# Rounded weights of the delta rule: GpSimd makes them per unit from raw weights, no longer per head in the table stage

## The chip, the cores and the metric

The kernel runs on one core of a Trainium2 chip. The metric is the device time of one execution in microseconds (us); a comparison takes the median of several executions. The engines are TensorE (PE in the views; PEld is its loading of weights), VectorE (DVE), ScalarE (ACT), GpSimd (POOL) and SyncE (SP), which here only issues transfers.

## What is computed

Input x has 8 sequences of 512 rows and 256 columns. Four blocks follow one another, each added to its own input:

```python
x = x + attn_a(layernorm(x))   # gated delta rule, 8 heads of 128, two key/value steps per row
x = x + ffn(layernorm(x))      # 256 -> 512 -> 512 -> 256, ReLU
x = x + attn_b(layernorm(x))   # attention, 16 heads, 4 key/value heads
x = x + ffn(layernorm(x))
```

The change concerns attn_a alone:

```python
q = silu(conv(x @ Wq)); k = silu(conv(x @ Wk)); v = silu(conv(x @ Wv))   # causal conv, 4 taps
q = l2norm(q) / sqrt(128); k = l2norm(k)
beta = 2 * sigmoid(x @ Wb); g = -exp(A_log) * softplus(x @ Wa + dt_bias)
for each row:                                   # per head, a state of 128 x 128
    state = state * exp(g)
    for j in (0, 1):
        state = state + k_j (v_j - k_j state)^T * beta_j
    o = q state
out = (rmsnorm(o) * norm_w * silu(x @ Wg)) @ Wo
```

## The kernel before

It is written engine by engine, with semaphores. Five stages run one after the other: `build_tables` (the table stage), `delta_rule`, a feed-forward stage, the second attention, and a feed-forward stage again. Within a stage each engine works through its own fixed list of instructions.

**float32 products in pieces.** A factor is split into a rounded piece `hi` (type float32r) and the rest, `lo` = value - `hi`; a product is hi*hi + hi*lo + lo*hi. In `project`, six matmuls (L571) make one 128 x 512 block from `w_hi`, `w_lo`, `x_hi` and `x_lo`.

**The table stage** loops over the 8 batches. VectorE takes statistics (L311), normalizes in four instructions of 128 x 256 (L320), TensorE transposes (L250), ScalarE copies the result out (L281, and rounded at L283), VectorE makes `lo` (L326), SP stores both pieces to xs_d in memory. VectorE waits for L283 before L326, so it begins the next batch behind it. Beside this loop GpSimd has its own over the heads' weights (`split_head`): SP loads a head's raw weights (128 x 1536, `load_head`), GpSimd multiplies by one into the rounded `wh_hi` (L230) and subtracts into `wh_lo` (L232), and SP stores both to ws_d (`store_head`, L179). There are nine such heads, the first one twice. Behind the loops come the gates (L330 to L352, beta and g for all heads) and one store of the tables, tab_d.

**The delta rule stage** loops over 64 units, a batch and a head each (`units`, `turn`); two batches of 8 units are one run of the loop. Sequences are cut into 8 chunks of 64 rows, 128 key rows each. In the turn of unit u TensorE, VectorE and ScalarE interleave three things by hand: the projections, convolutions and transposes of unit u, the levels of the inverse of a triangular matrix per chunk, and the chain over the chunks of an earlier unit (`chain_ks`, `chain_u`, `chain_s`: key times state, the update u, the new state). The parts that the prediction speaks of:

- SP's list per turn: the store of oT, the tables' row of the next unit (`g_tab`, L510), the weights of the next unit (`g_w_hi`, `g_w_lo`, L514, 768 KB each, and `g_taps`), then L stored to lower_d (L527) and read back as 16 x 16 blocks (`g_small`, L529), the inverted blocks stored (L535, 64 KB each), and read back as T (L538) and U (L540), 512 KB each. `sp.wait_ge` holds this list in order.
- GpSimd's list per turn (L1161 on): `g_dmt` masked (L1165), the sums for the next unit from `g_tab` (L1143, L1144), `bk2` (L1169, it needs the key norms that VectorE makes at L1045 and L1046), `g_dm` (L1170), `g_ctab` (L1171, L1172), then the substitution in the 16 x 16 blocks (L1152, L1154, some 30 short instructions) which waits for `g_small`, and `g_qg` (L1177).
- VectorE makes L from the Gram blocks and `g_dm` (L1011), and does the convolution's taps (L962).
- At the start GpSimd clears tiles (L1181, L1183), waits for VectorE's zeros (`d_zero2`) and raises the starting values of the semaphores (L1188).

Of the kernel before, what the change touches and what calls it, by code (L numbers as in the profile page):

```python
# [107 lines left out]
def build_tables(nc, io, sems):  # L108
# [3 lines left out]
    with ExitStack() as ctx:  # L112
# [51 lines left out]
        def _(sp):  # L164
# [8 lines left out]
            def load_head(h, par):  # L173
                sp.dma_start(wh[par][:], io["w_heads"][bass.ds(h, 1)].rearrange("a p k n c -> p (a k n) c")).then_inc(s[f"t_wh{par}"], 16)

            def store_head(h, par):
                sp.wait_ge(s["t_split"], 2 * h + 2)
                for i, piece in enumerate((wh_hi, wh_lo)):
                    sp.dma_start(io["ws_d"][bass.ds(h, 1), i:i + 1].rearrange("a i p n c -> p (a i n) c"),  # L179
                                 piece[par][:].bitcast(F32)).then_inc(s[f"t_ws{par}"], 16)  # L180

# [37 lines left out]
        @block.gpsimd  # L219
        def _(pool):  # L220
            nc.gpsimd.memset(eps[:], LN_EPS).then_inc(s["t_init"], 1)
            nc.gpsimd.memset(tab[:], 0.0).then_inc(s["t_init"], 1)
# [11 lines left out]
            pool.wait_ge(s["t_const"], 48)  # L234
            with pool.Fori(0, H // 2) as pair:
                for par in (0, 1):
                    split_head(pair * 2 + par, pair, par)
            split_head(H, H // 2, 0)
# [60 lines left out]
        def _(dve):  # L299
# [65 lines left out]
def delta_rule(nc, io, sems):  # L365
# [3 lines left out]
    with ExitStack() as ctx:  # L369
# [126 lines left out]
        def _(sp):  # L496
# [64 lines left out]
        def _(pe):  # L561
# [272 lines left out]
        def _(act):  # L834
# [43 lines left out]
            def turn(u, q, pair=None, b=None, hp=None, own=True, inverse=True):  # L878
# [48 lines left out]
                if own:  # L927
# [19 lines left out]
        def _(dve):  # L947
# [70 lines left out]
            def turn(u, q, pair=None, b=None, hp=None, own=True, inverse=True, base=None):  # L1018
# [1389 lines left out]
```

## Time and profile before

| | us |
|---|---|
| median of 3 runs | 4455.96 (4451.16 to 4456.58) |
| the profiled execution, its own time | 4464.27 |
| its span, first to last instruction | 4462.2 |
| table stage | 0 to 170 |
| delta rule stage | 170 to 2561 |
| mean granted clock of TensorE | 0.973 of full speed |

The profile is of one execution. Busy time in it is per engine and stage; an instruction's idle time before it is given with what released it, and a transfer with the time from its issue to its landing. In a timeline row the first number is the start and the second the time from the start to the end of the group in it.

### The profile page before, as it was taken

What the parts mean: (1) busy time and instruction counts of PE and PEld (TensorE: products, weight loads), DVE (VectorE), ACT (ScalarE), POOL (GpSimd) and SP (SyncE); (2) the same over time, 40 slices, a digit from 0 to 9 for tenths busy, and PEclk for the clock granted to TensorE, in tenths of its full rate; (3) what the DMA queues carried; (4) which work ended last, traced back from release to release, by engine and by line L of the source; (5) the groups of instructions that cost most, each with busy time, mean ns of one, the idle gap of its engine ahead of it and who ended that gap; (6) DMA issues with size and microseconds to landing.
All of it is one profiled execution on the core that took longest, in us unless ns stands there. A gap on an engine that the chain in (4) does not pass through costs nothing. (4 is left out here: it accounts for less than half of the span.)

```text
span 4462.2 us, 97071 instructions
## 1 busy us (share of the span) xinstructions
PE 4129.1 (93%) x32143; PEld 3442.7 (77%) x32143; DVE 3010.4 (67%) x7897; ACT 2183.5 (49%) x5660; POOL 1201.0 (27%) x2727
## 2 busy tenths in 40 slices
PE   3499999999999999999999779879999999999979
PEld 3388888888888888888888668767777777778768
DVE  5577777777777777777777345346776776776655
ACT  2255555555555555555555234334444444444344
POOL 5244444444444444444444100000000000000000
PEclk9999999999999999999999689979999999999989
DMA  6433433333333343333333132131111111111021
GB/s 253 150 100 101 120 114 106 106 102 109 100 110 99 107 123 106 104 110 100 109 100 101 59 134 85 41 98 41 38 51 52 52 32 52 52 47 42 15 68 34
DMA packets 558447, 393.06 MB, mean 88 GB/s; under 512 B 253040, under 2 KB 504944, under 8 KB 556400
## 3 DMA queue, kind: packets, MB, share of 16 engines
q1 hardware_dynamic: 557936, 386.69, 28.1%
q8 instruction: 267, 4.37, 0.4%
q14 instruction: 244, 2.00, 0.2%
HBM read 288.36 MB, written 98.14 MB: 87 GB/s over the span
## 5 line engine op out<-in xcount | busy, mean ns | idle before, releaser
L962 DVE SCALAR_TENSOR_TENSOR g_conv<-g_r,g_taps,g_conv 128x511 f32<-128x511 f32 (+2 forms) x961 | 700.0, 742 | 135.9 <-ACT g_conv L847 127.6
L851 ACT ACTIVATE g_us<-g_chn 128x128 f32<-128x128 f32 x528 | 146.6, 278 | 688.4 <-PE g_chn L646 687.6
L2001 ACT ACTIVATE a_pr<-a_pr,a_low 128x128 f32<-128x128 f32 (+3 forms) x512 | 286.6, 560 | 396.2 <-DVE a_low L2146 380.3
L1152 POOL TENSOR_TENSOR g_prod<-g_small 64x14 f32<-64x14 f32 (+6 forms) x896 | 227.0, 253 | 665.8 <-DMA g_small<-lower_d 600.2
L571 PE MATMUL g_r<-g_x_hi,g_w_hi 128*128 128x512 f32 x770 | 366.9, 477 | 9.6 <-issue 7.1
L2146 DVE CUSTOM_DVE_ANT_0 a_pr<-a_sc,a_bias 128x128 f32<-128x128 f32 (+3 forms) x512 | 242.2, 486 | 193.2 <-issue 174.2
L2306 POOL TENSOR_TENSOR a_dg<-a_const,a_fl 128x384 fp32r<-128x384 f32 x32 | 26.4, 826 | 1154.5 <-DVE a_fl L2153 1154.5
L571 PE MATMUL g_r<-g_x_hi,g_w_lo 128*128 128x512 f32 x770 | 306.8, 398 | 0.0
L571 PE MATMUL g_r<-g_x_lo,g_w_hi 128*128 128x512 f32 x770 | 305.0, 396 | 0.0
L1820 PE MATMUL a_out<-a_pt,a_v 128*128 128x512 f32 (+3 forms) x1024 | 297.9, 434 | 0.9 <-DVE a_oT L2166 0.9
L847 ACT ACTIVATE g_conv<-g_r,g_taps 128x512 f32<-128x512 f32 x321 | 220.4, 687 | 137.4 <-PE g_r L571 127.0
L1820 PEld LDWEIGHTS a_out<-a_pt,a_v 128*128 128x128 f32 x1024 | 185.0, 191 | 103.1 <-issue 62.6
L995 DVE SCALAR_TENSOR_TENSOR g_R<-g_chn,g_ctab,g_bv 128x128 f32<-128x128 f32 x462 | 160.4, 347 | 150.9 <-PE g_chn L638 136.7
L1154 POOL TENSOR_TENSOR g_small<-g_small,g_prod 64x14 f32<-64x14 f32 (+6 forms) x896 | 240.6, 269 | 70.3
L1828 PE MATMUL a_pb<-a_wo,a_oT 128*128 128x256 f32 x1024 | 231.8, 379 | 1.7 <-DVE a_oT L2166 0.9
L1003 DVE SCALAR_TENSOR_TENSOR g_S<-g_S,g_ctab,g_chn 128x128 f32<-128x128 f32 x396 | 137.2, 346 | 134.7 <-PE g_chn L656 134.7
L646 PE MATMUL g_chn<-g_R,g_U 128*128 128x128 f32 x924 | 213.9, 314 | 8.3 <-DVE g_R L995 6.9
L638 PE MATMUL g_chn<-g_S,g_kT 128*128 128x128 f32 x924 | 205.1, 304 | 13.8 <-DVE g_S L1001 10.9
L658 PE MATMUL g_ob<-g_us,g_at 128*128 128x128 f32 x1056 | 214.6, 286 | 0.4 <-ACT g_us L851 0.4
L987 DVE TENSOR_TENSOR g_U<-g_U,g_lev 64x128 f32<-64x128 f32 x520 | 147.8, 284 | 93.7 <-PE g_lev L611 88.2
L1828 PEld LDWEIGHTS a_pb<-a_wo,a_oT 128*128 128x128 f32 x1024 | 189.7, 190 | 25.3 <-DVE a_x L2186 1.2
L1745 PE MATMUL a_sc<-a_k_hi,a_q_hi 128*128 128x128 f32 (+3 forms) x512 | 185.4, 362 | 25.6 <-DVE a_low L2146 19.0
(355 smaller groups left out, 11714.6 us busy)
## 6 DMA issues: line engine op xcount, KB each, us to landing
g_w_hi<-ws_d SPq DMA_DIRECT2D x65, 768.0 KB, 5.5
g_w_lo<-ws_d SPq DMA_DIRECT2D x65, 768.0 KB, 6.7
lower_d<-g_L SPq DMA_DIRECT2D x64, 512.0 KB, 3.3
g_T<-low_d SPq DMA_DIRECT2D x64, 512.0 KB, 4.1
g_U<-upp_d SPq DMA_DIRECT2D x64, 512.0 KB, 5.4
a_w<-w_groups SPq DMA_DIRECT2D x32, 640.0 KB, 4.5
oT_d<-g_oT SPq DMA_DIRECT2D x67, 256.0 KB, 5.4
f_oT<-oT_d SPq DMA_DIRECT2D x8, 2048.0 KB, 9.4
```

The costliest lines, as they stand in the source:

```text
L571: mm = M.matmul(BANK[n][:], a[:, k, n, :], c[:, k, :], start=(i == 0), stop=(i == len(terms) - 1))
L638: M.matmul(chn[:, 0, :], keys[:, c, :], S[c % 2][:], start=True, stop=True).then_inc(s["d_ks"], 1)
L646: M.matmul(chn[:, 1, :], U[par][:, c, :], bv[par][:, 0, :] if c == 0 else R[:], start=True, stop=True).then_inc(s["d_u"], 1)
L658: mm = M.matmul(dst, at[(q + 2) % QN][:, c, :], us[:], start=(c % 2 == 0), stop=False)
L847: A(conv[TURN[n] % 2][:], BANK[n][:], ACT.Copy, scale=taps[par][:, n, CONV - 1:CONV]).then_inc(s["d_tap"], 1)
L962: ins = V.scalar_tensor_tensor(out=y[:, k:L], in0=x[:, 0:L - k], scalar=tap, in1=y[:, k:L], op0=ALU.mult, op1=ALU.add)
L1152: ch.link(G.tensor_tensor(prod[:, 0:SM - 1 - k, 0:k], small[:, k + 1:SM, k:k + 1].to_broadcast(shape), small[:, k:k + 1, 0:k].to_broadcast ...
L1154: ch.link(G.tensor_tensor(rest, rest, prod[:, 0:SM - 1 - k, 0:k], ALU.subtract))
L1820: mm = M.matmul(out[:, k * P:L], v[bp][:, k, at], pt[g % 2][:, first[k]:first[k] + L - k * P], start=(k == 0), stop=(k == TT - 1))
L1828: mm = M.matmul(pb[:, j * D:(j + 1) * D], oT[tp_][:, g, m * P:(m + 1) * P], wo[tp_][:, g, :], start=(g == 0), stop=(g == G - 1))
L2001: A(pr[g % 2][:, i, 0:width(i)], pr[g % 2][:, i, 0:width(i)], ACT.Exp, scale=-1.0, bias=low[g % 2][:, i:i + 1], accum_out=tot[g % 2][:, i: ...
L2146: V.tensor_tensor_reduce(pr[g % 2][:, i, 0:width(i)], sc[i % 2][:, 0:width(i)], bias[tp_][:, i, 0:width(i)], -SCALE, 3.0e38, ALU.add, ALU. ...
```

## The change

The table stage no longer handles heads' weights: `load_head`, `store_head` and `split_head` are gone, with their tiles and semaphores, and ws_d with them. The delta rule stage has a new tile `g_w_raw` (128 x 1536). SP loads a unit's raw weights from the input, two units ahead; GpSimd makes `w_hi` and `w_lo` of the next unit from it in every turn (`split_w`), 65 times in all with the first unit, whose `w_hi` is a copy by ScalarE and whose `w_lo` is made by GpSimd before its loop. TensorE waits for `d_wlo` instead of the transfer. The core of the diff:

```diff
@@ build_tables, gpsimd
-            def split_head(h, pair, par):
-                pool.wait_ge(s[f"t_wh{par}"], 16 * pair + 16)
-                pool.wait_ge(s[f"t_ws{par}"], 32 * pair + 1)
-                nc.gpsimd.tensor_tensor(wh_hi[par][:], wh[par][:], cc["ones"].unsqueeze(1).to_broadcast([P, KD * NB, P]), ALU.mult).then_inc(s["t_split"], 1)
-                pool.wait_ge(s["t_split"], 2 * h + 1)
-                nc.gpsimd.tensor_tensor(wh_lo[par][:], wh[par][:], wh_hi[par][:], ALU.subtract).then_inc(s["t_split"], 1)
...
@@ delta_rule, sync
-            def weights(h, par):
-                for i, piece in enumerate((w_hi, w_lo)):
-                    sp.dma_start(piece[par][:].rearrange("p k n c -> p (k n) c").bitcast(F32),
-                                 io["ws_d"][bass.ds(h, 1), i:i + 1].rearrange("a i p n c -> p (a i n) c")).then_inc(s[f"d_w{par}"], 16)
-                sp.dma_start(taps[par][:], io["taps"][bass.ds(h, 1)].rearrange("a p n t -> p (a n) t")).then_inc(s[f"d_w{par}"], 16)
+            def weights(h):
+                sp.dma_start(w_raw[:], io["w_heads"][h % H]).then_inc(s["d_wr"], 16)
+
+            def tap_rows(h, par):
+                sp.dma_start(taps[par][:], io["taps"][h % H]).then_inc(s[f"d_w{par}"], 16)
...
                 tables(u + 1, 1 - par)
-                sp.wait_ge(s["d_proj"], NB * u + 1)
                 sp.wait_ge(s["d_conv"], 5 * u + 1)
-                weights(hp * QN + q + 1, 1 - par)
+                tap_rows(hp * QN + q + 1, 1 - par)
...
                 for i, name in enumerate(("low_d", "upp_d")):
                     sp.dma_start(blocks_of(name), inv[:, i]).then_inc(s["d_XT"], 16)
+                sp.wait_ge(s["d_wlo"], u + 2)
+                weights(hp * QN + q + 2)
...
             rows(0)
+            sp.wait_ge(s["d_wlo"], 1)
+            weights(1)
             sp.wait_ge(s["d_zero2"], 1)
...
@@ delta_rule, tensor
-                    pe.wait_ge(s[f"d_w{1 - par}"], 48 * (pair + par) + 48)
+                    pe.wait_ge(s["d_wlo"], u + 2)
...
@@ delta_rule, scalar
+            act.wait_ge(s["d_wr"], 16)
+            A(w_hi[0][:], w_raw[:], ACT.Copy).then_inc(s["d_whi"], 1)
...
@@ delta_rule, gpsimd
+            def split_w(u, par):
+
+                raw, ones = w_raw[:].rearrange("p k n c -> p (k n) c"), cc["ones"].unsqueeze(1).to_broadcast([P, KD * NB, P])
+                pool.wait_ge(s["d_wr"], 16 * u + 16)
+                pool.wait_ge(s["d_proj"], NB * (u - 1) + 1)
+                hi, lo = (x[par][:].rearrange("p k n c -> p (k n) c") for x in (w_hi, w_lo))
+                G.tensor_tensor(hi, raw, ones, ALU.mult).then_inc(s["d_whi"], 1)
+                pool.wait_ge(s["d_whi"], u + 1)
+                G.tensor_tensor(lo, raw, hi, ALU.subtract).then_inc(s["d_wlo"], 1)
...
                 G.tensor_tensor(ctab[q][:, 1, :], tab[par][:, 2, :], cc["ones"][:, 0:NC], ALU.mult)
+                split_w(u + 1, 1 - par)
                 substitute(u)
...
+            pool.wait_ge(s["d_whi"], 1)
+            G.tensor_tensor(w_lo[0][:], w_raw[:], w_hi[0][:], ALU.subtract).then_inc(s["d_wlo"], 1)
             pool.wait_ge(s["d_zero2"], 1)
```

GpSimd's list in a turn of the delta rule, before (an ISA row stands for a wait; g_bk and g_rk are bk2 and rk2):

```order
L1169 TENSOR_TENSOR g_bk<-g_tab,g_rk 128x8
L96 ISA
L1170 TENSOR_TENSOR g_dm<-g_dm,g_bk 128x512
L1171 TENSOR_TENSOR g_ctab<-g_tab,g_rk 128x8
L1172 TENSOR_TENSOR g_ctab<-g_tab,g_const 128x8
L1148 ISA
L1152 TENSOR_TENSOR g_prod<-g_small 64x14
```

and with the change:

```order
L1155 TENSOR_TENSOR g_bk<-g_tab,g_rk 128x8
L96 ISA
L1156 TENSOR_TENSOR g_dm<-g_dm,g_bk 128x512
L1157 TENSOR_TENSOR g_ctab<-g_tab,g_rk 128x8
L1158 TENSOR_TENSOR g_ctab<-g_tab,g_const 128x8
L1125 ISA
L1126 ISA
L1128 TENSOR_TENSOR g_w_hi<-g_w_raw,g_const 128x1536
L1129 REGISTER_ALU
L1130 TENSOR_TENSOR g_w_lo<-g_w_raw,g_w_hi 128x1536
L1134 ISA
L1138 TENSOR_TENSOR g_prod<-g_small 64x14
```

The two splits stand between the last g_ctab and the first instruction that needs g_small; line numbers are lower by 14 there.

SP's list in a turn, from the tables' row on, before:

```order
L510 DMA g_tab<-tab_d 128x40
L523 ISA
L524 ISA
L514 DMA g_w_hi<-ws_d 128x1536
L514 DMA g_w_lo<-ws_d 128x1536
L516 DMA g_taps<-taps 128x20
L526 REGISTER_ALU
L527 DMA lower_d<-g_L 128x8x128
L528 ISA
L529 DMA g_small<-lower_d 64x16x16
L535 DMA low_d<-g_inv 64x16x16
L535 DMA upp_d<-g_inv 64x16x16
L536 REGISTER_ALU
L537 ISA
L538 DMA g_T<-low_d 128x8x128
L539 ISA
L540 DMA g_U<-upp_d 128x8x128
```

and with the change:

```order
L479 DMA g_tab<-tab_d 128x40
L492 ISA
L485 DMA g_taps<-taps 128x20
L494 REGISTER_ALU
L495 DMA lower_d<-g_L 128x8x128
L496 ISA
L497 DMA g_small<-lower_d 64x16x16
L503 DMA low_d<-g_inv 64x16x16
L503 DMA upp_d<-g_inv 64x16x16
L504 REGISTER_ALU
L482 DMA g_w_raw<-w_heads 128x1536
L506 ISA
L507 ISA
L508 DMA g_T<-low_d 128x8x128
L509 ISA
L510 DMA g_U<-upp_d 128x8x128
```

The two loads of weights behind g_tab are gone, and the raw load stands between the inverse's stores and T.

## Rows read from the trace of the kernel before

**Rows 1.** The page, busy time, share of the span and instructions of TensorE
```profile
PE 4129.1 (93%) x32143; PEld 3442.7 (77%) x32143; DVE 3010.4 (67%) x7897; ACT 2183.5 (49%) x5660; POOL 1201.0 (27%) x2727
```

**Rows 2.** Windows: length, then each engine's busy us, TensorE's clock, DMA share, GB/s
```profile
0.00:170.00 170.00, 53.51 (x330) 43.61 (x330) 88.85 (x150) 35.20 (x47) 64.30 (x31) 1.00 0.60 221
...
300.00:2300.00 2000.00, 1976.52 (x19255) 1656.75 (x19254) 1498.94 (x3404) 1135.88 (x3185) 871.09 (x2169) 1.00 0.36 107
```

**Rows 3.** Groups of the table stage: busy us, mean ns, then idle before
```profile
L320 DVE TENSOR_SCALAR t_xn<-t_x,t_mv,t_rstd 128x256 f32<-128x256 f32 x32 | 40.6, 1269 | 1.2
```

**Rows 4.** Single lines of VectorE: duration in ns, min/median/max, first and last start
```profile
L320 DVE TENSOR_SCALAR t_xn<-t_x,t_mv,t_rstd x32: 411/415/3458, 13.9 to 114.0; 128x256 f32<-128x256 f32 x32
...
L962 DVE SCALAR_TENSOR_TENSOR g_conv<-g_r,g_taps,g_conv x961: 732/741/752, 194.2 to 2485.5; 128x511 f32<-128x511 f32 x65, 128x509 f32<-128x509 f32 x64, 128x510 f32<-128x510 f32 x64
...
L1011 DVE TENSOR_TENSOR g_L<-g_lev,g_dm x128: 679/681/692, 208.7 to 2466.0; 128x512 f32<-128x512 f32 x128
...
L1045 DVE TENSOR_SCALAR g_ss<-g_ss x64: 160/658/1047, 204.5 to 2461.3; 128x8 f32<-128x8 f32 x64
```

**Rows 5.** Timeline, first batches: start us, us, engine, line; GpSimd, then VectorE
```profile
12.89 3.42 POOL L230 TENSOR_TENSOR t_wh_hi<-t_wh,t_const 128x1536 fp32r<-128x1536 f32 x1 [9.65 <-DMA t_wh<-w_heads]
...
23.30 3.42 POOL L232 TENSOR_TENSOR t_wh_lo<-t_wh,t_wh_hi 128x1536 fp32r<-128x1536 f32 x1
...
13.90 12.96 DVE L320 TENSOR_SCALAR t_xn<-t_x,t_mv,t_rstd 128x256 f32<-128x256 f32 x4
...
32.03 1.80 DVE L311 BATCH_NORM_STATS2 t_stats<-t_x 128x6 f32<-128x256 f32 x4
...
34.83 1.76 DVE L320 TENSOR_SCALAR t_xn<-t_x,t_mv,t_rstd 128x256 f32<-128x256 f32 x4
...
41.77 1.80 DVE L311 BATCH_NORM_STATS2 t_stats<-t_x 128x6 f32<-128x256 f32 x4
```

**Rows 6.** DMA issues of 0 to 195 us: KB, median us to landing
```profile
t_x<-x SPq DMA_DIRECT2D x8, 512.0 KB, 4.5
```

**Rows 7.** Timeline, start of the delta rule stage: SP's queue, then GpSimd
```profile
171.30 0.42 SPq L514 DMA_DIRECT2D g_w_hi<-ws_d  x1
...
180.47 0.20 POOL L1183 MEMSET g_qden<- 128x4 f32 x4
...
184.04 0.82 POOL L1188 MEMSET g_scrap<- 128x1 f32 x23 [3.38 <-DVE g_scrap L1122]
```

**Rows 8.** DMA issues of 300 to 2300 us: KB, median us to landing
```profile
g_w_hi<-ws_d SPq DMA_DIRECT2D x56, 768.0 KB, 5.5
...
g_taps<-taps SPq DMA_DIRECT2D x56, 10.0 KB, 7.3
```

**Rows 9.** Waits of 300 to 2300 us: total, times, longest
```profile
POOL g_prod L1152 <- DMA g_small<-lower_d: 522.8, 56, 10.4
```

**Rows 10.** Timeline of a unit (GpSimd, VectorE), and the narrowest wait for g_small
```profile
1277.93 1.04 POOL L1170 TENSOR_TENSOR g_dm<-g_dm,g_bk 128x512 f32<-128x512 f32 x1
...
1279.10 0.20 POOL L1172 TENSOR_TENSOR g_ctab<-g_tab,g_const 128x8 f32<-128x8 f32 x1
...
1288.62 0.21 POOL L1152 TENSOR_TENSOR g_prod<-g_small 64x14 f32<-64x14 f32 x1 [9.32 <-DMA g_small<-lower_d]
...
1280.92 1.28 DVE L1011 TENSOR_TENSOR g_L<-g_lev,g_dm 128x512 f32<-128x512 f32 x2
...
789.33 0.21 POOL L1152 TENSOR_TENSOR g_prod<-g_small 64x14 f32<-64x14 f32 x1 [7.27 <-DMA g_small<-lower_d]
```

**Rows 11.** Timeline of SP's queue in the same unit
```profile
1265.06 0.68 SPq L535 DMA_DIRECT2D upp_d<-g_inv  x1
...
1268.24 0.39 SPq L538 DMA_DIRECT2D g_T<-low_d  x1
```

**Rows 12.** Windows around it: the last number is what the DMA engines moved, GB/s
```profile
1267.00:1269.00 2.00, 2.00 (x13) 1.52 (x12) 1.93 (x5) 0.99 (x3) 0.00 (x0) 1.00 0.11 14
...
1274.00:1277.00 3.00, 3.00 (x27) 2.96 (x27) 2.61 (x5) 2.21 (x13) 1.74 (x2) 1.00 1.05 428
```

More of the change, by code:

```diff
@@ L145, in build_tables @@
         start = sb("t_start", [P, 8])
-        wh = [sb(f"t_wh{i}", [P, KD * NB, P]) for i in (0, 1)]
-        wh_hi, wh_lo = ([sb(f"t_wh_{n}{i}", [P, KD * NB, P], F32R) for i in (0, 1)] for n in ("hi", "lo"))
         ps_x = ps("t_ps_x", [P, 2, L])
@@ L171, in load_x @@
                 sp.dma_start(x[par][:], io["x"][bass.ds(b, 1)].rearrange("a (m p) d -> p (a m) d", p=P)).then_inc(s[f"t_x{par}"], 16)
[L173 to L180, printed above, removed]
             def store_rows(b, par):
@@ L192, in turn @@
                 store_rows(b, par)
-                store_head(b, par)
-                if more or par == 0:
-                    load_head(b + 2, par)
             load_x(1, 1)
-            load_head(0, 0)
-            load_head(1, 1)
             with sp.Fori(0, B // 2 - 1) as pair:
@@ L205, in _ @@
             store_rows(B, 1)
-            store_head(H, 0)
-            sp.wait_ge(s["t_ws0"], 32 * (H // 2 + 1) + 1)
-            sp.wait_ge(s["t_ws1"], 32 * (H // 2) + 1)
             sp.wait_ge(s["t_glo"], 1)
@@ L222, in _ @@
             nc.gpsimd.memset(tab[:], 0.0).then_inc(s["t_init"], 1)
-            for i, name in enumerate(("t_out0", "t_out1", "t_tr", "t_sig", "t_ws0", "t_ws1", "t_xlo")):
+            for i, name in enumerate(("t_out0", "t_out1", "t_tr", "t_sig", "t_xlo")):
                 nc.gpsimd.memset(start[:, i:i + 1], 0.0).then_inc(s[name], 1)
-            def split_head(h, pair, par):
-                pool.wait_ge(s[f"t_wh{par}"], 16 * pair + 16)
-                pool.wait_ge(s[f"t_ws{par}"], 32 * pair + 1)
-                nc.gpsimd.tensor_tensor(wh_hi[par][:], wh[par][:], cc["ones"].unsqueeze(1).to_broadcast([P, KD * NB, P]), ALU.mult).then_inc(s["t_split"], 1)
-                pool.wait_ge(s["t_split"], 2 * h + 1)
-                nc.gpsimd.tensor_tensor(wh_lo[par][:], wh[par][:], wh_hi[par][:], ALU.subtract).then_inc(s["t_split"], 1)
[L234 to L238, printed above, removed]
         @block.tensor
@@ L356 @@
 T_SEMS = ["t_const", "t_x0", "t_x1", "t_xT", "t_out0", "t_out1", "t_tab", "t_init", "t_xn", "t_tr", "t_ab", "t_g", "t_sum", "t_A",
-          "t_mv", "t_std", "t_sig", "t_beta", "t_abs", "t_exp", "t_dec", "t_dve", "t_wh0", "t_wh1", "t_ws0", "t_ws1", "t_split", "t_xlo", "t_xhi", "t_glo", "t_move"]
+          "t_mv", "t_std", "t_sig", "t_beta", "t_abs", "t_exp", "t_dec", "t_dve", "t_xlo", "t_xhi", "t_glo", "t_move"]
 K0, K1, V0, V1, QB, GB = range(6)
@@ L385, in delta_rule @@
         x_hi, x_lo = (sb(f"g_x_{i}", [P, KD, L], F32R) for i in ("hi", "lo"))
+        w_raw = sb("g_w_raw", [P, KD, NB, P])
         w_hi, w_lo = (some(2, f"g_w_{i}", [P, KD, NB, P], F32R) for i in ("hi", "lo"))
@@ L540, in turn @@
                 sp.dma_start(U[par][:], chunks_of("upp_d")).then_inc(s["d_TU"], 16)
-            weights(0, 0)
+            weights(0)
+            tap_rows(0, 0)
             tables(0, 0)
             rows(0)
+            sp.wait_ge(s["d_wlo"], 1)
+            weights(1)
             sp.wait_ge(s["d_zero2"], 1)
@@ L554, in _ @@
                 store(u)
-            sp.wait_ge(s["d_w0"], 48 * (UNITS // 2 + 1))
+            sp.wait_ge(s["d_w0"], 16 * (UNITS // 2 + 1))
+            sp.wait_ge(s["d_wr"], 16 * (UNITS + 2))
             sp.wait_ge(s["d_tab0"], 16 * (UNITS // 2 + 1))
@@ L825, in _ @@
             pe.wait_ge(s["d_x"], 32)
-            pe.wait_ge(s["d_w0"], 48)
+            pe.wait_ge(s["d_wlo"], 1)
             pe.wait_ge(s["d_at"], 1)
@@ L931, in turn @@
                     ins.then_inc(s["d_qsq"], 1)
-                    act.wait_ge(s[f"d_w{1 - par}"], 48 * (pair + par) + 48)
+                    act.wait_ge(s[f"d_w{1 - par}"], 16 * (pair + par) + 16)
                     first_tap(u + 1, 1 - par, K0)
                     A(tiny[:], tiny[:], ACT.Silu)
+            act.wait_ge(s["d_wr"], 16)
+            A(w_hi[0][:], w_raw[:], ACT.Copy).then_inc(s["d_whi"], 1)
             act.wait_ge(s["d_zero"], 1)
@@ L939, in _ @@
             decay_start(0, 0)
-            act.wait_ge(s["d_w0"], 48)
+            act.wait_ge(s["d_w0"], 16)
             first_tap(0, 0, K0)
@@ L1104, in turn @@
                 if own:
-                    dve.wait_ge(s[f"d_w{1 - par}"], 48 * (pair + par) + 48)
+                    dve.wait_ge(s[f"d_w{1 - par}"], 16 * (pair + par) + 16)
                     convolve(u + 1, 1 - par, K0, 1, 2)
@@ L1126, in _ @@
             ch.turn(0)
-            dve.wait_ge(s["d_w0"], 48)
+            dve.wait_ge(s["d_w0"], 16)
             convolve(0, 0, K0, 1, 2)
@@ L1193, in _ @@
             units(pool, turn)
-D_SEMS = ["d_const", "d_zero", "d_zero2", "d_x", "d_w0", "d_w1", "d_tab0", "d_tab1", "d_store", "d_blank", "d_Ls", "d_D", "d_X", "d_XT", "d_TU", "d_sub",
+D_SEMS = ["d_const", "d_zero", "d_zero2", "d_x", "d_w0", "d_w1", "d_wr", "d_whi", "d_wlo", "d_tab0", "d_tab1", "d_store", "d_blank", "d_Ls", "d_D", "d_X", "d_XT", "d_TU", "d_sub",
           "d_proj", "d_tap", "d_rep", "d_gm", "d_dm", "d_exp", "d_conv", "d_silu", "d_gate", "d_ktr", "d_ksq", "d_rk2", "d_rk",
@@ L2397 @@
         io[name] = nc.dram_tensor(name, (NC * (P * P + P),), F32).ap()
-    io["ws_d"] = nc.dram_tensor("ws_d", (H + 1, 2, P, KD * NB, P), F32).ap()
     io["keep_d"] = nc.dram_tensor("keep_d", (HKV * L,), F32).ap()
```

## The prediction

> **What bounds the kernel now.** I read the page first: TensorE is busy for 93% of the span [rows 1]. That share mixes stages, so the second view is the table of windows [rows 2]. In the delta rule stage (from 170 us; 300 to 2300 is its steady part) TensorE is busy for 1976.52 of 2000 us: all its waits together come to 23.5 us, 0.42 for each of the 56 units in it. There nothing that VectorE, GpSimd or a queue gives back is worth more than that 0.42 a unit, while what makes TensorE wait costs in full. The table stage (0 to 170 us) is the opposite: TensorE 53.51, VectorE 88.85, GpSimd 64.30 of 170. No engine is full; the time is that of a chain from one batch's rows to the next.
>
> The third view, the groups of that stage, shows the longest link [rows 3]: 32 normalizing instructions of VectorE at L320, 40.6 us in all, 1269 ns each. The view of that line alone gives 411 ns at the least, 415 as the median and 3458 at the most [rows 4]. The timeline shows why [rows 5]: GpSimd's splits L230 and L232 take 3.42 us each and run back to back from 12.89 to 26.7; beside them L320's four instructions take 12.96 us, and each of them that is caught lasts about as long as a split. In the next batch no split runs beside them, and the four take 1.76. GpSimd looks as if it worked beside the chain; it stands in it.
>
> **The table stage.** Nine heads' splits go (18 instructions on GpSimd), and on SP nine loads and eighteen stores of 768 KB. The price of the splits is what they do to L320: 40.6 less 32 x 0.415 = 13.3 leaves **27.3 us**. It lies on the chain, since VectorE starts a batch (L311) only behind L326 of the last one, and that waits for ScalarE's L283, TensorE's L250 and L320 in turn. The undisturbed batch takes 9.74 us from L311 to L311, 32.03 to 41.77 [rows 5]. What is late next? A batch's rows land 4.5 us after their issue [rows 6], and they are issued more than a batch of 9.74 ahead of their use, so the load does not take over. Behind the loop a few VectorE instructions of the gates could gain a little too; I count nothing for them, nor for the stores into ws_d, which are no part of the chain.
>
> The rule behind this is in the Trainium skill, "SBUF — State Buffer", in its part on the engine and DMA sides: VectorE and GpSimd share one pair of ports under an exclusive lock, whichever starts first keeps it for its whole instruction, and VectorE needs it for instructions in a two-port mode or with two SBUF tensors as inputs. The trace agrees at L320, with 3458 ns for the longest. By the rule and by the rows the sum is the same; what the rule adds is which instructions to look for in the units.
>
> **The start of the delta rule stage.** Added are a raw load, a ScalarE copy of it into w_hi and one GpSimd subtraction, 3.42 us by its twin L232. GpSimd has cleared its tiles by 180.67, and L1188, which lets the others begin, starts at 184.04 [rows 7]; between them it waits for VectorE's zeros. The raw tile is issued where g_w_hi is now, at 171.30, and such a load lands in 5.5 us [rows 7, 8], which leaves 3.9 us for a copy of 1536 columns before GpSimd is free. So the subtraction fills 180.7 to 184.1, and L1188 comes **0.1 us** later. The bounds are nothing and the whole 3.4, if load or copy ran that late. SP now sends the second raw load ahead of the zeros for low_d and upp_d, but TensorE's first product waits for GpSimd's gsum and not for them.
>
> **The steady units, GpSimd.** Each unit gets two instructions of 3.42 us, 6.9 for the pair (12.89 to 26.7 are two pairs, [rows 5]), between L1172 and L1152. There GpSimd waits for g_small, 522.8 us in 56 units or 9.3 each [rows 9]. In the unit shown L1172 ends at 1279.30; the split would end at 1286.2 and g_small releases L1152 9.32 us after L1172's end, at 1288.62: 2.4 us to spare. The narrowest of the stage's 64 waits is 7.27 [rows 10], and holds it too. I cost both instructions at **nothing**; what hides them is the round trip of lower_d through memory. Without that cover each unit's inverse would come up to 6.9 us later, and with it L1177's g_qg, for which TensorE waits in chain_s. The new wait of TensorE for d_wlo is met long before: the split ends near 1286, and K0 of the next unit comes at the end of the unit.
>
> **The steady units, VectorE.** Can the split stop it there as in the table stage? From 1279.3 to 1286.2 it runs L1003, L1015, L995, L1011, L962 and L974, each with an operand in PSUM. None of these is ever stretched beside GpSimd's instructions of 1.04 us: L962 takes 732 to 752 ns in 961 instructions, L1011 679 to 692 [rows 4]. The one that is stretched is L1045, a small tensor_scalar from SBUF to SBUF: 160 to 1047 ns, the length of L1143 or L1144. But GpSimd's L1169 waits for what follows from it, so the split always comes behind it. Cost: **nothing**; the rivals have the bound.
>
> **The steady units, SP's queue.** 1.5 MB of w_hi and w_lo, now behind the tables' row g_tab, go; 768 KB of raw weights come in ahead of T, U, the store of oT and g_tab. SP has nothing to do between upp_d (1265.06 + 0.68) and T (1268.24) [rows 11], and from 1267 to 1269 the DMA engines move 14 GB/s [rows 12]. 786 kB at 428 GB/s, the rate of the weights now [rows 12], take 1.84 us, so the raw load would run from about 1267.2 to 1269.1, when T's packets begin. I take **no delay** for g_tab. It has room: dm (L1170) ends at 1278.97 and L1011, which needs it, starts at 1280.92, 1.95 us later [rows 10].
>
> **The sum.** 27.3 - 0.1 = 27.2 us less. The profiled execution took 4464.27 us (span 4462.2), so it would be 4437.1. The median of the runs shown is 4455.96, 8.3 below the profiled one; 27.2 less is **4428.8**. A measurement of this kernel can tell about 0.2%, or 9 us.
>
> **The rivals.**
> - *g_tab comes late* (slower). It is in the queue behind the raw load now. For it: g_taps, 10 KB, lands 7.3 us after its issue behind the weights [rows 8]. T's issue hangs on the landing of the inverse's stores, which the fast load beside them could put off. If the raw load did not fit in front of T at all, its 1.84 us and an issue of 1 us would delay g_tab by 2.84 us, and L1011 by what exceeds the room of 1.95: 0.89 x 64 = 57 us, so 4455.96 - 27.2 + 57 = 4486. It makes the kernel slower from a delay of 2.4 us on (1.95 + 27.2/64). Against it: the idle stretch of the engines. Chance 6%.
> - The Trainium skill, "DMA: Bandwidth & Descriptors", on queues and completion order, has the general form: on each DMA engine descriptors are consumed in ring order. It gives this rival no time.
> - *The split stops VectorE in the units* (slower). One instruction caught per unit waits 1.7 us on average, half of 3.42: x 64 = 109, so 4538. For it: L320 and L1045. Against it: no candidate in the stretch. Chance 3%.
> - *The small collision changes its phase.* L1045 takes 658 ns in the median and 160 when it misses L1143 and L1144, which start when g_tab lands. A g_tab that moves by half a microsecond could make it always miss, 0.5 x 64 = 32 us of VectorE's time (TensorE's idle 0.42 a unit allows 27 of them), or always hit in full, (1.05 - 0.66) x 64 = 25 more. I know no reason for either end. Half of each, -13 and +13, belongs to the forecast's range; the whole ends, 4402 and 4454, have 4% and 3%.
> - *The table stage hangs on something else* (no change): a store of xs_d or a load that L320 hides now. Against it: the undisturbed batch of 9.74 us, with all that traffic. About 4456, chance 3%.
>
> **How the numbers follow.** The forecast case keeps 81%. Its range is 4428.8 less 13, and plus 13 and up to 3 for the start: 4415 to 4445, which leaves the rivals' ends out, 19%. Faster by over 0.2% are the forecast and the lucky phase, 0.85; within 0.2% the unlucky phase and the table stage's rival, 0.06; slower the first two rivals, 0.09.
>
> **What would show it.** In the changed profile L288, the old L320, should take 0.41 to 0.42 us in all 32, and the delta rule stage should begin near 143 us. In the units L1128 and L1130 should take 3.42 us each and end before g_small releases L1138; TensorE should still be busy for 98.8% of the steady part, and g_tab land 4.5 us after its issue. L1011's or L962's successors stretched, or waiting for dm, or TensorE idle for more than 0.42 us a unit, would prove me wrong.

## The result and the profile after

| | median us | lowest to highest |
|---|---|---|
| before, 6 runs | 4458.02 | 4451.16 to 4465.96 |
| after, 6 runs | 4430.25 | 4422.1 to 4432.91 |
| after over before | 0.9932 | 95%: 0.9921 to 0.9942 |

The change takes 27.8 us off by the medians; the interval of the ratio allows 26 to 35. The sum had said 27.2, and the predicted time was 4428.8. The profiled execution of after has a span of 4428.5. The one of before (4462.2) is itself some 6 us slower than its median, so the two spans differ by 33.7, which is more than the change is worth; stages are compared below with that in mind.

The page of after first, its row of busy times, which answers to [rows 1]:

```profile
PE 4126.1 (93%) x32143; PEld 3443.9 (78%) x32143; DVE 2977.5 (67%) x7897; ACT 2185.5 (49%) x5661; POOL 1582.6 (36%) x2836
```

GpSimd is busy for 381.6 us more than before, VectorE for 32.9 less, and the kernel is faster: the share of an engine says nothing of where its work lies. The windows of the two stages (answering to [rows 2]; the table stage ends 29 us earlier, so its window does too):

```profile
0.00:142.00 142.00, 53.49 (x330) 43.60 (x330) 61.58 (x151) 35.21 (x47) 3.46 (x13) 1.00 0.32 115
300.00:2300.00 2000.00, 1973.20 (x19274) 1657.92 (x19270) 1497.54 (x3411) 1138.31 (x3196) 1259.43 (x2288) 1.00 0.33 85
```

In the steady part TensorE is busy for 1973.20 of 2000 us against 1976.52: nearly as full as before, but not fuller.

**The table stage.** The line of the normalizing instruction (L288 now), which answers to [rows 4]:

```profile
L288 DVE TENSOR_SCALAR t_xn<-t_x,t_mv,t_rstd x32: 411/412/415, 13.3 to 86.0; 128x256 f32<-128x256 f32 x32
```

None of the 32 is longer than 415 ns; before, 12 of them were, with 972 to 3458 ns, and their excess adds up to the 27.3 us. The timeline shows the first batches (as [rows 5]) and the last `lo` (L294), and behind it the last `lo` of before:

```profile
10.47 1.81 DVE L279 BATCH_NORM_STATS2 t_stats<-t_x 128x6 f32<-128x256 f32 x4 [10.47 <-ACT t_heads L242]
...
13.27 1.76 DVE L288 TENSOR_SCALAR t_xn<-t_x,t_mv,t_rstd 128x256 f32<-128x256 f32 x4
...
20.20 1.80 DVE L279 BATCH_NORM_STATS2 t_stats<-t_x 128x6 f32<-128x256 f32 x4
...
29.93 1.80 DVE L279 BATCH_NORM_STATS2 t_stats<-t_x 128x6 f32<-128x256 f32 x4
...
40.75 1.80 DVE L279 BATCH_NORM_STATS2 t_stats<-t_x 128x6 f32<-128x256 f32 x4
...
90.42 1.22 DVE L294 TENSOR_TENSOR t_x_lo<-t_ps_x,t_x_hi 128x1024 fp32r<-128x1024 f32 x1 [4.03 <-ACT t_x_hi L251]
```

```profile
118.46 1.23 DVE L326 TENSOR_TENSOR t_x_lo<-t_ps_x,t_x_hi 128x1024 fp32r<-128x1024 f32 x1 [4.03 <-ACT t_x_hi L283]
```

A batch now takes 9.73 us, the undisturbed batch of before, from the first one on; three of them, as before, take 10.8, since ScalarE loads a table first (1.28 us). The last `lo` starts 28.0 us earlier.

**The start of the delta rule stage.** Timeline of SP's queue and GpSimd, answering to [rows 7]:

```profile
142.45 0.33 SPq L482 DMA_DIRECT2D g_w_raw<-w_heads  x1
...
151.45 3.44 POOL L1172 TENSOR_TENSOR g_w_lo<-g_w_raw,g_w_hi 128x1536 fp32r<-128x1536 f32 x1
154.81 0.84 POOL L1177 MEMSET g_scrap<- 128x1 f32 x23
```

The one subtraction fills the gap of 3.38 us that GpSimd had in front of this memset. L1177 starts at 154.81, 29.2 us earlier than L1188 did.

**A steady unit.** SP's queue, then GpSimd, then VectorE (answering to [rows 10, 11]; the last row of GpSimd is the first instruction of the block substitution):

```profile
1235.38 0.58 SPq L503 DMA_DIRECT2D low_d<-g_inv  x1
...
1236.79 0.59 SPq L482 DMA_DIRECT2D g_w_raw<-w_heads  x1
1238.76 0.38 SPq L508 DMA_DIRECT2D g_T<-low_d  x1
...
1239.96 2.26 SPq L471 DMA_DIRECT2D oT_d<-g_oT  x1
1242.48 0.36 SPq L479 DMA_DIRECT2D g_tab<-tab_d  x1
...
1246.64 1.04 POOL L1119 TENSOR_TENSOR g_gsum<-g_tab,g_const 128x512 fp32r<-128x512 f32 x1 [8.82 <-DMA g_tab<-tab_d]
...
1248.93 1.04 POOL L1156 TENSOR_TENSOR g_dm<-g_dm,g_bk 128x512 f32<-128x512 f32 x1
...
1250.26 3.46 POOL L1128 TENSOR_TENSOR g_w_hi<-g_w_raw,g_const 128x1536 fp32r<-128x1536 f32 x1
1253.80 3.46 POOL L1130 TENSOR_TENSOR g_w_lo<-g_w_raw,g_w_hi 128x1536 fp32r<-128x1536 f32 x1
1259.31 0.21 POOL L1138 TENSOR_TENSOR g_prod<-g_small 64x14 f32<-64x14 f32 x1 [2.05 <-DMA g_small<-lower_d]
...
1251.29 1.28 DVE L987 TENSOR_TENSOR g_L<-g_lev,g_dm 128x512 f32<-128x512 f32 x2
```

The splits lie in the wait for g_small, which still ends last, by 2.05 us here. But one row is not as before: the store of oT takes 2.26 us of SP's time where it took 1.03, and g_tab comes behind it. The waits of 300 to 2300 us (total, times, longest) show what follows from that, first in after, then in before:

```profile
POOL g_gsum L1119 <- DMA g_tab<-tab_d: 510.1, 56, 10.9
POOL g_prod L1138 <- DMA g_small<-lower_d: 91.1, 55, 3.6
...
DVE g_L L987 <- POOL g_dm L1156: 9.5, 10, 1.3
```

```profile
POOL g_gsum L1143 <- DMA g_tab<-tab_d: 462.5, 56, 12.0
...
DVE g_L L1011 <- POOL g_dm L1170: 2.7, 2, 1.5
```

The wait for g_small went from 522.8 us [rows 9] to 91.1. GpSimd's wait for g_tab grew from 462.5 to 510.1, 0.85 us a unit, and VectorE now waits for dm 10 times, 9.5 us in all, where before it did twice, 2.7 us.

### The profile page after: what moved, and what is told of

Its sections match the earlier page's. It is cut to its first block and busy times, and to the rows that moved or that the text cites. A ratio compares the mean times of both kernels' runs of the same rounds, so it can differ in the third digit from the quotient of the medians.

```text
span 4428.5 us, 96953 instructions
## 1 busy us (share of the span) xinstructions
PE 4126.1 (93%) x32143; PEld 3443.9 (78%) x32143; DVE 2977.5 (67%) x7897; ACT 2185.5 (49%) x5661; POOL 1582.6 (36%) x2836
## 5 line engine op out<-in xcount | busy, mean ns | idle before, releaser
L938 DVE SCALAR_TENSOR_TENSOR g_conv<-g_r,g_taps,g_conv 128x511 f32<-128x511 f32 (+2 forms) x961 | 699.0, 741 | 133.9 <-ACT g_conv L821 125.4
L1119 POOL TENSOR_TENSOR g_gsum<-g_tab,g_const 128x512 fp32r<-128x512 f32 x65 | 68.1, 1047 | 580.1 <-DMA g_tab<-tab_d 580.0
L1130 POOL TENSOR_TENSOR g_w_lo<-g_w_raw,g_w_hi 128x1536 fp32r<-128x1536 f32 x64 | 221.0, 3453 | 5.0
L1128 POOL TENSOR_TENSOR g_w_hi<-g_w_raw,g_const 128x1536 fp32r<-128x1536 f32 x64 | 221.4, 3459 | 0.0
```

Source lines behind the costliest of these rows:

```text
L938: ins = V.scalar_tensor_tensor(out=y[:, k:L], in0=x[:, 0:L - k], scalar=tap, in1=y[:, k:L], op0=ALU.mult, op1=ALU.add)
L1128: G.tensor_tensor(hi, raw, ones, ALU.mult).then_inc(s["d_whi"], 1)
L1130: G.tensor_tensor(lo, raw, hi, ALU.subtract).then_inc(s["d_wlo"], 1)
```

## The experiments

All are edits of after, if nothing else is said. Ratios are to the kernel before, run beside each.

| run | what | median us | ratio | 95% |
|---|---|---|---|---|
| e1 | GpSimd's splits back in the table stage | 4462.47 | 1.0007 | 0.9995 to 1.0019 |
| e2 | only the transfers back | 4430.92 | 0.9936 | 0.9921 to 0.995 |
| e3 | units' splits cut to 8 columns | 4426.32 | 0.992 | 0.9906 to 0.9935 |
| e4 | no raw loads in the units | 4430.55 | 0.994 | 0.9927 to 0.9953 |
| e5 | raw load behind the taps | 4431.34 | 0.993 | 0.9917 to 0.9943 |
| e6 | tables' row ahead of T | 4420.08 | 0.991 | 0.9897 to 0.9923 |
| e7 | e5 and e6 together | 4421.55 | 0.9913 | 0.9899 to 0.9926 |
| e8 | kernel **before**, tables' row ahead of T | 4450.67 | 0.9976 | 0.9967 to 0.9985 |
| e9 | a third split instruction per unit | 4547.01 | 1.0192 | 1.0177 to 1.0207 |
| e11 | e9 with the tables' row ahead of T | 4440.05 | 0.9949 | 0.9935 to 0.9964 |

### Was it the splits or the transfers?

e1 puts the 18 instructions back, on a tile that GpSimd fills itself, with no load and no store:

```diff
+            nc.gpsimd.memset(wh[:], 1.0).then_inc(s["t_split"], 1)
+            pool.wait_ge(s["t_const"], 48)
+            for h in range(H + 1):
...
+                nc.gpsimd.tensor_tensor(wh_hi[:], wh[:], cc["ones"].unsqueeze(1).to_broadcast([P, KD * NB, P]), ALU.mult).then_inc(s["t_split"], 1)
...
+                nc.gpsimd.tensor_tensor(wh_lo[:], wh[:], wh_hi[:], ALU.subtract).then_inc(s["t_split"], 1)
```

> The changed kernel with the nine pairs of 3.42 us put back on GpSimd in the table stage, on a tile that GpSimd fills itself, with no load and no store of them. Theory (GpSimd's instructions themselves stop VectorE's L288 lines, by the shared ports): the 18 run back to back for some 62 us, every normalizing instruction that falls into that time takes about 3.4 us, a batch takes 20.9 us instead of 9.7 for about three batches, so the kernel is about 33 us slower than the changed one, near 4463 us. Rival (the weights' transfers slowed the stage): no normalizing instruction is stretched and the time stays near 4430.

Measured: 4462.47, ratio 1.0007. The whole gain is gone, and the 32 us over after are more than the 27.8 because the splits run back to back here. The normalizing line of e1, then the timeline of its first batches:

```profile
L298 DVE TENSOR_SCALAR t_xn<-t_x,t_mv,t_rstd x32: 411/414/3461, 13.2 to 118.6; 128x256 f32<-128x256 f32 x32
```

```profile
10.43 1.81 DVE L289 BATCH_NORM_STATS2 t_stats<-t_x 128x6 f32<-128x256 f32 x4 [10.43 <-ACT t_heads L252]
13.24 12.92 DVE L298 TENSOR_SCALAR t_xn<-t_x,t_mv,t_rstd 128x256 f32<-128x256 f32 x4
...
31.34 1.80 DVE L289 BATCH_NORM_STATS2 t_stats<-t_x 128x6 f32<-128x256 f32 x4
34.13 13.03 DVE L298 TENSOR_SCALAR t_xn<-t_x,t_mv,t_rstd 128x256 f32<-128x256 f32 x4
```

Here the splits wait for no load and run back to back to 71.5 us, and the first three batches take 21 us each instead of 9.73. Once the splits are over, the batches are as long as in after. So GpSimd's instructions do it, with no transfer of the weights at all.

e2 is the counterpart: the nine loads and eighteen stores are back, the splits are not.

```diff
+                store_head(b, pair, par)
+                if more or par == 0:
+                    load_head(b + 2, par)
```

> The changed kernel with the nine loads and eighteen stores of 768 KB put back on SP in the table stage, and no splits. Theory: all 32 normalizing instructions stay at 0.41 us and the time within 2 us of the changed kernel's 4430; the heads' row at the start lands 0.6 us later, as it did before. Rival (the transfers were the cause): the stage is longer by up to 27 us, 4457.

Measured: 4430.92, the time of after, with all 32 instructions at 411 to 416 ns. In the table stage the rows t_x land 5.4 us after their issue instead of 3.9, and nobody waits for that. The one small detail expected of the start was wrong: the first batch starts at 9.97 us, earlier than in after (10.47). The 27 transfers of 768 KB were worth nothing in time.

### Do the units pay for the splits?

```diff
-                G.tensor_tensor(hi, raw, ones, ALU.mult).then_inc(s["d_whi"], 1)
+                cut = lambda t: t[:, 0:1, 0:8]
+                G.tensor_tensor(cut(hi), cut(raw), cut(ones), ALU.mult).then_inc(s["d_whi"], 1)
...
-                G.tensor_tensor(lo, raw, hi, ALU.subtract).then_inc(s["d_wlo"], 1)
+                G.tensor_tensor(cut(lo), cut(raw), cut(hi), ALU.subtract).then_inc(s["d_wlo"], 1)
...
```

> The changed kernel with the units' two splits cut to 8 columns each (so the product uses weights that are not the unit's); all transfers stay. Theory (the splits are hidden in the wait for the small blocks): within 5 us of the changed kernel's 4430, GpSimd's wait for the small blocks back at some 8.5 us a unit. Rival (they cost something in the units): faster by 10 us or more. The table's row should come as late as in the changed kernel, since that is not GpSimd's doing.

Measured: 4426.32, 4 us under after, with runs from 4415.64 to 4438.48; that is inside the scatter, so the 128 instructions of 3.46 us, 443 us of GpSimd, cost nothing that can be told apart here. GpSimd's wait for g_small is back at 462.4 us. The raw load is still there, and GpSimd waits as long for g_tab as in after (504.7 us in the steady part, 510.1 in after); but VectorE waits for dm only twice, 0.4 us. So the waits for dm need the splits too, and are not the raw load's doing alone.

### Does the raw load in front of T delay the units?

e4 leaves the units' raw loads out (of the two ahead of the loop, the first stays); e5 keeps them, but behind the taps:

```diff
                 tap_rows(hp * QN + q + 1, 1 - par)
+                sp.wait_ge(s["d_wlo"], u + 1)
+                weights(hp * QN + q + 1)
...
-                sp.wait_ge(s["d_wlo"], u + 2)
-                weights(hp * QN + q + 2)
```

> The changed kernel without the raw loads in the units: every unit splits the first head's weights (the product uses the wrong head's). Theory (the raw load ahead of T fills the queue and delays what SP issues behind it): T lands 4.1 us after its issue instead of 5.0, the store of oT is issued in 0.7 us instead of 1.5 to 2.9, the table's row starts GpSimd's sums about 1.1 us earlier in the unit, VectorE waits for dm in 1 or 2 units instead of 16, and the small tensor_scalar of the key norms is caught more often again (0.58 us on average instead of 0.37). In time the two cancel: within 6 us of 4430. Rival (the raw load costs more than the collision gives): 10 us faster or more.

> The changed kernel with the raw load moved: behind the taps in the unit's own turn, one unit ahead instead of two. Theory: the queue ahead of T is free again, so T lands 4.1 us after its issue, the store of oT is issued in under 1.1 us and the table's row is issued 1.1 us earlier; the key norms' instruction is caught for 0.55 to 0.6 us again and VectorE waits for dm in at most 2 units; GpSimd's split is not delayed by more than a microsecond, which its wait for the small blocks covers. Time within 6 us of the changed kernel's 4430. Rival (the raw load lands too late for the split, and the inverse is late): slower by 10 us or more.

Measured: 4430.55 and 4431.34, both the time of after. Yet the queue did change. The line of the oT store shows how long SP is held at it, in ns (min/median/max); before, after, e4:

```profile
L502 SPq DMA_DIRECT2D oT_d<-g_oT x67: 333/898/2413, 188.6 to 2561.5; - x67
```

```profile
L471 SPq DMA_DIRECT2D oT_d<-g_oT x67: 332/1757/3259, 163.8 to 2527.8; - x67
```

```profile
L471 SPq DMA_DIRECT2D oT_d<-g_oT x67: 332/904/2041, 159.8 to 2528.6; - x67
```

And T lands in 4.1 us (median) in before, e4 and e5, in 5.1 in after. So the raw load costs 1 us at T and 0.85 at the store, and with it g_tab is late by about as much as GpSimd's longer wait. Why is that free? The group of the small instruction of VectorE (busy us, mean ns, idle before; 300 to 2300 us) in before and in after:

```profile
L1045 DVE TENSOR_SCALAR g_ss<-g_ss 128x8 f32<-128x8 f32 x56 | 32.7, 584 | 0.0
```

```profile
L1021 DVE TENSOR_SCALAR g_ss<-g_ss 128x8 f32<-128x8 f32 x56 | 20.2, 361 | 0.0
```

With g_tab later, GpSimd's pair of sums starts later and catches this instruction less often (27 of 64 times, 46 before): 12.5 us of VectorE's time come back, 6.8 go into waits for dm. In e4 the dm waits are gone and the instruction is back at 527 ns over all 64 units (571 before, 362 after). That is one reading: two effects, of a few us each and opposite in sign, and the time stands still. e4 alone does not tell it from the other, that neither reaches the time. A third small instruction, L1092 (L1116 before), takes 469 ns on average after and 373 before, 6.1 us in all; but in e1, whose units are those of after, it takes 378, so it moves by as much from one execution to the next.

### Moving the sums away from the small instruction

If that is so, a g_tab that comes much earlier should gain on both. e6 loads the tables' row of two units ahead in front of T (tab_d gets one row more, and the row of unit 1 is loaded ahead of the loop):

```diff
                 store(u)
-                sp.wait_ge(s["d_bv"], 2 * u + 2)
-                tables(u + 1, 1 - par)
...
                 weights(hp * QN + q + 2)
+                sp.wait_ge(s["d_bv"], 2 * u + 4)
+                tables(u + 2, par)
```

> The changed kernel with the table's row loaded a turn earlier, ahead of T, behind the raw load. Theory (where the row lands decides what is left of the waits in a unit): GpSimd's two sums of 1.04 us then run some 4 us before the key norms' instruction, which takes 0.16 us in all units, and dm is ready before the Gram blocks in all: the unit's period goes from 35.6 to 35.35 to 35.45 us, 10 to 16 us less, 4414 to 4420. Rival (TensorE's own work sets the period and VectorE's small waits cost nothing): within 4 us of 4430.

> Both moves: the table's row ahead of T and the raw load behind the taps. Theory: as with the row moved alone, 4414 to 4420, and T lands in 4.1 us; T's landing was not on the path, so nothing more than 3 us comes from it. Rival: the raw load behind the taps makes the split late, and some of the gain is lost.

> The kernel before the change with its table's row loaded ahead of T. Theory (the small instruction of the key norms, caught by GpSimd's sums for 0.59 us a unit, and nothing that the change brought, is what the move gives back): 8 to 14 us less than the kernel before. Rival (the gain of the moved row was the repair of the change's own lateness, 16 units that wait for dm): within 4 us of the kernel before.

Measured: e6 4420.08, e7 4421.55, and e8, the same move in the kernel before, 4450.67 beside 4462.26. e6 beats both kernels, after by 10 us; it was not run beside after itself, but beside e5, which has after's time, and that is 11 us slower. The intervals of the ratios of e6 and e5 just overlap; that of e8 lies clear of 1. The small instruction in e6, and what TensorE waits for in the chain (300 to 2300 us):

```profile
L1023 DVE TENSOR_SCALAR g_ss<-g_ss x64: 160/161/165, 175.4 to 2422.4; 128x8 f32<-128x8 f32 x64
```

```profile
PE g_chn L614 <- DVE g_S L979: 11.7, 22, 1.0
```

It is never caught again, and no unit waits for dm. Over the 64 units e6 gives VectorE back 12.8 us at this instruction (23.2 less 10.4) and 9.5 of dm waits, and gains 10; e8 gives back 26.3 (36.6 less 10.3) and gains 11.6. So somewhat under half of what VectorE gets back here reaches TensorE. By that rate the change's own shift, 12.5 less 6.8 in the steady part, is worth 3 us, too little to be measured. e7 and e8 show that the gain has to do with the sums' place and not with the raw load or with the change.

### How much room have the splits?

e9 issues the `hi` instruction twice, 3.45 us more per unit:

```diff
+                for k in range(1):
+                    G.tensor_tensor(hi, raw, ones, ALU.mult).then_inc(s["d_ex"], 1)
+                    pool.wait_ge(s["d_ex"], 1 * (u - 1) + k + 1)
                 G.tensor_tensor(hi, raw, ones, ALU.mult).then_inc(s["d_whi"], 1)
```

> The changed kernel with the first instruction of the split done twice in every unit: 3.45 us more of GpSimd per unit. The loop that GpSimd closes: key norms ready, bk2 and dm and ctab 1.65 us, split, substitution to g_qg 13.1, TensorE's chain_s and the next unit up to its key norms 9.2, with waits 0.4. With 10.4 us of splits that is 34.8 of a period of 35.6, so the theory says hidden: within 6 us of 4430, with the inverse's blocks stored up to 2 us later in the unit. Rival (any lateness of the inverse reaches TensorE): 1.9 us x 64 = 120 us slower.

Measured: 4547.01, 117 us over after. The theory fell and the rival, 120 us, was right. I had counted the wait for g_small and some work behind the substitution as slack. Timeline of a unit of e9, GpSimd with SP's queue between (the second row of g_qg is a unit later):

```profile
1254.47 1.27 POOL L1167 TENSOR_TENSOR g_qg<-g_qT,g_gam 128x512 f32<-128x512 f32 x1
...
1266.06 1.04 POOL L1119 TENSOR_TENSOR g_gsum<-g_tab,g_const 128x512 fp32r<-128x512 f32 x1 [9.09 <-DMA g_tab<-tab_d]
...
1269.68 3.44 POOL L1129 TENSOR_TENSOR g_w_hi<-g_w_raw,g_const 128x1536 fp32r<-128x1536 f32 x1
...
1280.15 0.21 POOL L1141 TENSOR_TENSOR g_prod<-g_small 64x14 f32<-64x14 f32 x1
...
1292.01 1.26 POOL L1167 TENSOR_TENSOR g_qg<-g_qT,g_gam 128x512 f32<-128x512 f32 x1
```

```profile
1254.54 0.58 SPq L503 DMA_DIRECT2D low_d<-g_inv  x1
...
1257.85 0.38 SPq L508 DMA_DIRECT2D g_T<-low_d  x1
...
1260.84 0.45 SPq L479 DMA_DIRECT2D g_tab<-tab_d  x1
```

This is a closed loop. The inverse's end (X) lets SP store low_d, T waits for that store, the oT store and g_tab stand behind T in SP's list, g_tab releases GpSimd's sums, behind them come the splits, then the substitution, then the next X. In e9 it takes 11.6 + 3.6 + 10.5 + 11.9 = 37.6 us, the length of its unit. In the unit of after shown above the same sum is 11.3 + 3.6 + 7.05 + 11.9 = 33.9, and a unit takes 35.6 (median): 1.7 us of room. The 91.1 us in 56 units that GpSimd still waits for g_small, 1.6 each, say the same. The third instruction, 3.45, exceeds it by 1.75, times 64 is 112, against 117 measured.

e11 cuts the loop at its link through T: e9 with e6's move.

> The third instruction of the split in every unit as before, and the table's row loaded ahead of T. New theory: the loop that closed at 37.3 us goes from the inverse's store over SP's list to the table's row (11.3 us), GpSimd's sums, bk2, dm and ctab (3.6), the splits (10.5) and the substitution (11.9); the table's row ahead of T takes some 6 us out of it, and what is left is under the 35.5 us of TensorE. So the 117 us are gone: 4420 to 4432. Rival (the inverse's lateness itself reaches TensorE, by T and U or by g_qg): the time stays above 4500.

Measured: 4440.05. Of the 117 us 107 are gone, so the loop was what bound e9. But it is 20 over e6 (17 by the two ratios), and 8 over the upper end that I gave. The wait of TensorE in e11, as the row of e6 above, then another small instruction of VectorE (L1094) in e11 and in e6:

```profile
PE g_chn L614 <- DVE g_S L979: 32.3, 52, 1.0
```

```profile
L1094 DVE TENSOR_SCALAR g_qden<-g_ssq x64: 149/782/1198, 201.8 to 2468.2; 128x4 f32<-128x4 f32 x64
```

```profile
L1094 DVE TENSOR_SCALAR g_qden<-g_ssq x64: 149/168/1190, 201.6 to 2448.7; 128x4 f32<-128x4 f32 x64
```

The timeline of e11 shows it between GpSimd's g_qg and g_dmt:

```profile
1276.41 1.29 POOL L1169 TENSOR_TENSOR g_qg<-g_qT,g_gam 128x512 f32<-128x512 f32 x1
1277.66 1.28 POOL L1156 TENSOR_TENSOR g_dmt<-g_dmt,g_const 128x512 f32<-128x512 f32 x1
```

```profile
1278.19 0.78 DVE L1094 TENSOR_SCALAR g_qden<-g_ssq 128x4 f32<-128x4 f32 x1
...
1280.97 0.28 DVE L979 COPY g_S<-g_chn 128x128 f32<-128x128 f32 x1
```

GpSimd's wait for g_small, 3.0 us a unit in e6, takes up most of the third instruction, and in e11 nearly none of it is left (2.4 us in all). The rest moves GpSimd's list by some 0.6 us, so that g_dmt, which starts 1.07 us ahead of L1094 in e6, starts 0.45 ahead of it and catches it in 62 of 64 units for 26; its mean goes from 389 to 791 ns, 25.7 us over the units, and the copy of the state behind it is late for TensorE: 32.3 us of waiting in 2000 for 11.7. The growth of either fits the 17 to 20 us. That it is all of them was not tried on its own; an e11 with L1094 moved would show it.

## Why the prediction was right, and where it was not

**The table stage: right, mechanism and size.** Forecast 27.3. The last `lo` comes 28.0 us earlier: 27.4 of it is L320's excess (40.6 less 13.2), and 0.6 is that the first batch starts sooner, behind the heads' row. The 0.6 is no work of the change: with all the transfers of the weights, it starts at 9.97 us in e2 and 10.57 in e8, for 11.09 in before and 10.47 in after. e1 brings all of it back with the splits alone, e2 none of it with the transfers alone. The rival that the stage hangs on something else is out.

**The gates behind the loop: right at "a little".** L298, the instruction on t_beta, takes 0.69 instead of 1.05 us, and by the first load of the next stage the lead is 29.2 us, not 28.0. These 1.2 us I had set at nothing. 0.4 is this instruction; the lead is 28.5 us at the first store of tab_d (134.35 for 162.86), and the last 0.7 come between these stores and the next stage's first load (141.19 for 170.43). Their cause is open.

**The start of the delta rule stage: right.** Raw load, copy and subtraction fit in front of L1177. It comes 29.2 us earlier, as the first load does: the cost was under 0.1.

**The rest of the span.** From this memset to the last instruction of the chain (L1089 before, L1065 after) it is 2373.5 us before and 2368.9 after, and from there to the end 1904.8 in both. The 4.6 us are about what before's profiled execution is over its median. The lead at the memset is 29.2 us and the medians differ by 27.8, so by the medians the units are as long as they were, within some 1.4 us.

**GpSimd in the units: right in time, wrong in its reason.** The splits take 3.46 us, not 3.42, and cost nothing that stands out of the scatter (e3). The prediction named the round trip of lower_d as their cover and found 2.4 us to spare in the unit shown. It missed that the splits lengthen a loop that comes back to them through SP's list and g_tab, and held the narrowest wait of 7.27 to be the limit. The room that is left is 1.7 us, and e9 pays for what exceeds it.

**VectorE in the units: right.** L938 stays at 731 to 752 ns and L987 at 677 to 693, beside splits of 3.46 us. The rule of the Trainium skill, "SBUF — State Buffer", that the lock concerns instructions in a two-port mode or with two SBUF inputs, is borne out on both sides: these two have an operand in PSUM and are never caught, while L1094 of e6 and e11, from SBUF to SBUF, goes from 149 to 1198 ns. That L1094 runs in a two-port mode is inferred; no view tells it.

**SP's queue: the step that failed.** "I take no delay for g_tab": GpSimd's first sum, which waits for it, starts 11.6 us after the issue of low_d's store on average, for 10.7 before, and in e4 10.4. 0.2 us of this is there when T is issued, the store of oT adds the most. The prediction let the raw load's packets run from 1267.2 to 1269.1 of before's unit at 428 GB/s, so it had them begin some 1.3 us after the issue. Windows of after, where the raw load is issued at 1236.79 and T at 1238.76 (last number GB/s):

```profile
1238.00:1239.00 1.00, 1.00 (x6) 0.68 (x5) 0.96 (x4) 0.19 (x2) 0.00 (x0) 1.00 1.23 162
1239.00:1240.00 1.00, 1.00 (x9) 0.85 (x8) 0.97 (x2) 0.96 (x3) 0.00 (x0) 1.00 0.91 344
1240.00:1241.00 1.00, 0.92 (x6) 0.48 (x4) 1.00 (x3) 0.73 (x2) 0.00 (x0) 1.00 0.93 325
```

The full rate comes only from 1239 on, 2.2 us after the issue and when T is queued already, and it is some 330 GB/s. The delay stayed under the room of 1.95 us that the prediction had measured, in most units: VectorE waits for dm in 13 of 64, 12.1 us in all (2 before, 2.7). By the prediction's own signs this step was wrong: L987 waits for dm, and TensorE is idle for 26.8 us of the steady part, 0.48 a unit and not 0.42. That is the rival of a late g_tab, at under half the delay from which it would decide. The other rival, the small collision's phase, acted as well and the other way, by 13.4 us of VectorE's time (36.6 to 23.2) and, at e6's rate, some 6 of the kernel's. The two about cancel by that rate, and e4 and e5, which undo both, take after's time: the sum was right by more luck than its working tells, within the range that the collision had been given. That it hit to 0.6 us is luck as well, with an interval of 26 to 35 us on the difference.

## What to carry to other kernels

A busy GpSimd is not free where VectorE has short instructions from SBUF to SBUF on the chain: look at the maximum of a line beside its median, and place GpSimd's work where VectorE's operands lie in PSUM or where nobody waits for it. An idle stretch of an engine is room only to the point where the loop through it, the queues' order included, is as long as the period; add up that loop before you fill the stretch. When a shift of one event changes nothing, look for two effects of opposite sign, since one of them may be had alone, as e6 did for 10 us.

## What the runs showed of the hardware

**Tiny instructions pay whole ones.** VectorE's instruction on 128 x 8 elements takes 160 ns alone and up to 1047 beside a GpSimd instruction of 1.04 us; one on 128 x 4 takes 149 and up to 1198 beside one of 1.28 in e6 (1324 is the most in after); one on 128 x 256 takes 411 and up to 3461 beside one of 3.4. The largest excess follows GpSimd's length and not VectorE's work. In e9 one on 128 x 4 took 2591 while GpSimd's instructions of 0.73, 0.87 and 1.28 us followed one another directly.

**Issuing a DMA can take SP microseconds.** The store of oT takes SP 0.33 us when nothing is in flight ahead of it and up to 3.26 when the raw load, T and U are; the median goes from 0.90 to 1.76 with the raw load and back to 0.90 without it (e4). SP's list stands still meanwhile, so what is behind it is later than the order of the list tells. What limit is met there no run shows. That T lands in 5.1 and not 4.1 us behind the raw load goes with the Trainium skill, "DMA: Bandwidth & Descriptors", on queues and completion order: descriptors of one queue are consumed in ring order on each DMA engine.

**GpSimd hardly pays.** Its split takes 3.42 us in the table stage, where it catches VectorE's instructions, and 3.46 in the units, where no VectorE instruction beside one of the 128 is stretched. In these collisions it is VectorE that is stretched.
